# A gated network on one core: silu made on ScalarE directly, in place of a tanh there and one operation on VectorE

## What is computed

```python
x = x + jnp.tanh(g_xattn[0]) * L0_xattn(layernorm(x), ctx)   # RWKV-style weighted scan
x = x + jnp.tanh(g_ffn[0])   * L0_ffn(layernorm(x))
x = x + jnp.tanh(g_xattn[1]) * L1_xattn(layernorm(x), ctx)   # linear attention, sigmoid gate
x = x + jnp.tanh(g_ffn[1])   * L1_ffn(layernorm(x))
# inside L0_ffn: a dense MLP and 8 of 512 product-key experts per token
mlp = silu(x @ gate_w) * (x @ up_w) @ down_w                  # 256 -> 1024 -> 256
ew  = silu(einsum('nh,nkh->nk', x, de)) * softmax(scores)
# inside L1_ffn: 8 routed experts, 2 per token, and a shared one, hidden width 128
h      = silu(rin @ w1[e].T) * (rin @ w3[e].T)
shared = silu(xf @ sw1.T) * (xf @ sw3.T) @ sw2.T
```

## Time and profile before

| | |
|---|---|
| median of 3 runs | 586.26 us (586.02 to 588.57) |
| the profiled execution | 589.14 us, its span 587.3 us |
| mean granted TensorE clock in it | 0.92 |
| busy: PE, DVE, ACT, POOL | 81%, 68%, 30%, 25% of the span |

### The profile page before, as it was taken

One profiled execution on the slowest core, in us unless ns is written; L12 is line 12 of the kernel. 1 busy time (PEld: TensorE's weight loads), 2 busy tenths in 40 slices (PEclk: granted clock), 3 DMA queues, 4 the chain that ended last, 5 costly groups with the idle time before them and its releaser, 6 DMA issues.

```text
span 587.3 us, 7047 instructions
## 1 busy us (share of the span) xinstructions
PE 477.8 (81%) x2142; PEld 367.5 (63%) x2150; DVE 402.3 (68%) x1049; ACT 173.8 (30%) x363; POOL 144.1 (25%) x141
## 2 busy tenths in 40 slices
PE   1755989778999679899999979999868599999720
PEld 1432468656767567668776867777646487888510
DVE  6999777999868997867859683997825343223332
ACT  2601434121233111141222123213334147555210
POOL 4942113551104010000000010000275105004664
PEclk9857999989999889989999989999978699999775
DMA  8150012300000049000000000111121416555653
GB/s 296 69 186 0 2 30 93 94 1 0 2 0 1 1 135 304 1 1 0 2 1 0 2 0 28 54 55 54 64 90 71 127 36 195 165 168 171 180 182 123
DMA packets 34277, 43.79 MB, mean 75 GB/s; under 512 B 3009, under 2 KB 28098, under 8 KB 34242
## 3 DMA queue, kind: packets, MB, share of 16 engines
q1 hardware_dynamic: 31170, 34.96, 18.6%
q0 software_dynamic: 3072, 8.39, 4.7%
HBM read 24.99 MB, written 18.35 MB: 74 GB/s over the span
## 4 chain that ended last, share of the span: by engine, by line
PE 36%; issue 6%; POOL 5%; DVE 4%; DMA 3%; ACT 2%; POOLq 0%; SPq 0%; ACTq 0%; DVEq 0%
PE ring L600 6%; PE acc L564 5%; PE ring L751 3%; PE ring L820 2%; PE ring L767 2%; PE ring L619 2%; PE ring L540 2%; POOL x_rows L1456 2%; PE ring L541 2%; PE ring L542 2%; PE ring L800 2%; POOL q_f L1465 2%; PE ring L584 1%; DMA main_b<-x_rows 1%; PE ring L811 1%
## 5 line engine op out<-in xcount | busy, mean ns | idle before, releaser
L564 PE MATMUL acc<-w_down,act_s 128*128 128x256 f32 x384 | 91.0, 384 | 0.7 <-DVE act_s L1258 0.7
L564 PEld LDWEIGHTS acc<-w_down,act_s 128*128 128x128 f32 x384 | 73.9, 193 | 12.7 <-DVE act_s L1258 1.1
L540 PE MATMUL ring<-xt_h,up_l 128*128 128x512 f32 x160 | 72.3, 452 | 5.4 <-ACT logits L921 3.0
L1426 POOL TENSOR_TENSOR rstd<-var_eps,minus_half 128x4 f32<-128x4 f32 x16 | 16.6, 1035 | 215.5 <-DVE var_eps L1054 215.5
L541 PE MATMUL ring<-xt_l,up_h 128*128 128x512 f32 x160 | 65.0, 406 | 0.0
L542 PE MATMUL ring<-xt_h,up_h 128*128 128x512 f32 x160 | 64.9, 406 | 0.0
L971 ACT ACTIVATE act_s<-ring 128x512 f32<-128x512 f32 x48 | 28.7, 598 | 113.8 <-PE ring L542 113.8
L1241 DVE SCALAR_TENSOR_TENSOR act_s<-act_s,ring 128x512 f32<-128x512 f32 x48 | 32.7, 681 | 29.4 <-ACT act_s L971 22.6
L600 PE MATMUL ring<-up_e,act_s 128*128 x184 | 48.4, 409 | 4.7 <-issue 3.5
L1456 POOL DMA_INDIRECT x_rows<-main_a,slots x32 | 31.5, 985 | 64.5 <-ACT main_a L988 32.4
L600 PEld LDWEIGHTS ring<-up_e,act_s 128*128 128x128 f32 x184 | 35.7, 204 | 11.3 <-issue 6.9
(11 more groups left out here) (239 smaller groups left out, 948.6 us busy)
## 6 DMA issues: line engine op xcount, KB each, us to landing
main_b<-x_rows SPq DMA_DIRECT2D x22, 256.0 KB, 2.9
y_rows<-act_s SPq DMA_DIRECT2D x22, 256.0 KB, 2.2
x_rows<-k_r SPq DMA_DIRECT2D x1, 3968.0 KB, 14.5
x_nat<-in_x SPq DMA_DIRECT2D x8, 256.0 KB, 4.5
stage<-in_w_mlp SPq DMA_DIRECT2D x8, 256.0 KB, 2.7
up_e<-in_w_moe SPq DMA_DIRECT2D x8, 256.0 KB, 2.6
out_x<-x_nat SPq DMA_DIRECT2D x8, 256.0 KB, 2.3
x_rows<-k_r SPq DMA_DIRECT2D x1, 1920.0 KB, 19.7
```

What stands on the lines that cost most here:

```text
L540: pe.matmul(out, wl, xh, start=first, stop=False, skip_group_check=True)
L564: last = pe.matmul(acc[t // 2][:, t % 2, :], act_s[n % RING][:, tok], w_down[:, u, :], start=u == 0 and t % 2 == 0, stop=final, skip_group ...
```

## The change

ACT uses the function Silu on bank A and releases the bank itself; DVE's operation (t + 1) * A is gone in all three places, and with it the halving of the gates. In the units 8 to 11 DVE waits for the silu only ahead of its last multiplication. The semaphores tanh_ready and shared_tanh are gone, since the release of the bank now tells DVE that the silu is written; block_tanh is renamed.

```diff
--- before.py
+++ after.py
@@ -412,20 +412,18 @@
         exp_ready = sem("exp_ready")
         routes_ready = sem("routes_ready")
         exps_high = sem("exps_high")
-        tanh_ready = sem("tanh_ready")
         hid_ready = sem("hid_ready")
         down_done = sem("down_done")
         acc_free = sem("acc_free")
         gate_ready = sem("gate_ready")
         chosen_ready = sem("chosen_ready")
-        shared_tanh = sem("shared_tanh")
         shared_ready = sem("shared_ready")
         slots_ready = sem("slots_ready")
         rows_scaled = sem("rows_scaled")
         rows_cleared = sem("rows_cleared")
         row_sent = [sem(f"row_sent{k}") for k in range(SENDS)]
         blocks_loaded = [sem(f"blocks_loaded{k}") for k in range(4)]
-        block_tanh = sem("block_tanh")
+        block_silu = sem("block_silu")
         y_stored = [sem(f"y_stored{k}") for k in range(2)]
         y_back = [sem(f"y_back{k}") for k in range(2)]
         y_added = sem("y_added")
@@ -968,14 +966,15 @@
                             act.wait_ge(down_done, n - RING + 1)
                         elif n == 0:
                             act.wait_ge(bg_ready, 1)
-                        act.activation(act_s[n % RING][:, :], bank[:, :], ACT.Tanh, scale=0.5).then_inc(tanh_ready, 1)
+                        act.activation(act_s[n % RING][:, :], bank[:, :],
+                                       ACT.Silu).then_inc(free_sem((step, "A", u)), 1)
                         if u == IC:
                             hidden_made(act, n - 1)
                             bank = full(act, (step, "EY"))
                             act.activation(host_s[:, 0, :], bank[:, :], ACT.Copy).then_inc(free_sem((step, "EY")), 1)
                 elif kind == "moe":
                     bank = full(act, (step, "A"))
-                    act.activation(hid_shared[g], bank[:, :], ACT.Tanh, scale=0.5).then_inc(shared_tanh, 1)
+                    act.activation(hid_shared[g], bank[:, :], ACT.Silu).then_inc(free_sem((step, "A")), 1)
                 elif kind == "send":
                     t = part
                     main = t // GT
@@ -1004,8 +1003,8 @@
                             full(act, (("blk", n - 3), "H"))
                         wide = pair_blocks(n - 1)
                         act.activation(hid_blocks[(n - 1) % 2][:, 0:wide * P].rearrange("p (j m) -> p j m", j=wide),
-                                       bank[:, 0:wide * 2 * P].rearrange("p (j m) -> p j m", j=wide)[:, :, 0:P], ACT.Tanh,
-                                       scale=0.5).then_inc(block_tanh, 1)
+                                       bank[:, 0:wide * 2 * P].rearrange("p (j m) -> p j m", j=wide)[:, :, 0:P],
+                                       ACT.Silu).then_inc(block_silu, 1)
                     if 2 <= n <= PAIRS + 1:
                         key = (("blk", n - 2), "H")
                         bank = full(act, key)
@@ -1091,7 +1090,6 @@
                     dve.tensor_tensor(bias_b[:, :], bias_b[:, :], bias_a[:, :], ALU.add).then_inc(dve_setup, 1)
                     dve.wait_ge(act_setup, 2)
                     dve.wait_ge(pool_setup, 1)
-                    dve.tensor_scalar(gates[:, 1::2], gates[:, 1::2], 0.5, None, ALU.mult)
                     for c in range(C):
                         last = dve.tensor_copy(decay[:, c, :].rearrange("p (t j) -> p t j", t=GT)[:, :, 1:],
                                                ew[:, c:c + 1].unsqueeze(2).broadcast_to([P, GT, P]))
@@ -1236,13 +1234,12 @@
                     n = unit_of(g, u)
                     s = act_s[n % RING]
 
-                    dve.wait_ge(tanh_ready, n + 1)
-                    bank = full(dve, (step, "A", u))
-                    free((step, "A", u), dve.scalar_tensor_tensor(s[:, :], s[:, :], 1.0, bank[:, :], ALU.add, ALU.mult))
                     if u >= IC:
                         if u == IC:
                             freed(dve, (step, "EY"))
                         w = host_s[:, 1, :]
+                        if HID_TURN[("mlp", g, u)] > 1:
+                            dve.wait_ge(hid_ready, HID_TURN[("mlp", g, u)] - 1)
 
                         bank = full(dve, (step, "RANK", u))
                         free((step, "RANK", u), dve.scalar_tensor_tensor(w, bank[:, :], float(TOPK), host_s[:, 0, :],
@@ -1253,6 +1250,7 @@
                             bank = full(dve, (step, "OVER"))
                             free((step, "OVER"), dve.tensor_tensor(w, w, bank[:, :], ALU.add))
 
+                        freed(dve, (step, "A", u))
                         for a in range(2):
                             r = slice(a * 2 * P, (a + 1) * 2 * P)
                             last = dve.tensor_tensor(s[:, r].rearrange("p (j h) -> p h j", h=2),
@@ -1329,9 +1328,7 @@
                     dve.wait_ge(chosen_ready, g + 1)
                 elif kind == "moe":
                     a = hid_shared[g]
-                    dve.wait_ge(shared_tanh, g + 1)
-                    bank = full(dve, (step, "A"))
-                    free((step, "A"), dve.scalar_tensor_tensor(a, a, 1.0, bank[:, :], ALU.add, ALU.mult))
+                    freed(dve, (step, "A"))
                     bank = full(dve, (step, "B"))
                     dve.tensor_tensor(a, bank[:, :], a, ALU.mult).then_inc(free_sem((step, "B")), 1)
                     freed(dve, (step, "B"))
@@ -1382,8 +1379,7 @@
                         bank = full(dve, (("blk", n), "U"))
                         both = bank[:, 0:wide * 2 * P].rearrange("p (j w m) -> p j w m", j=wide, w=2)
                         a = hid_blocks[n % 2][:, 0:wide * P].rearrange("p (j m) -> p j m", j=wide)
-                        dve.wait_ge(block_tanh, n + 1)
-                        link(dve.scalar_tensor_tensor(a, a, 1.0, both[:, :, 0, :], ALU.add, ALU.mult))
+                        dve.wait_ge(block_silu, n + 1)
                         dve.tensor_tensor(a, both[:, :, 1, :], a, ALU.mult).then_inc(free_sem((("blk", n), "U")), 1)
                 elif kind == "gather":
                     q = part
```

## The result

Four runs of each kernel: the changed one takes 579.02 us (578.19 to 580.18), the one before 586.68 us (586.02 to 588.57). The medians differ by 7.7 us; the ratio is 0.9859, 95% interval 0.9837 to 0.9881, so 1.4% faster. The forecast was 579.2.

What follows compares the result with a forecast made beforehand. TensorE, 81% busy, was taken to be held up to 410 us by waits on VectorE. Stretch terms -0.9 - 2.9 + 0.8 - 2.1 - 2.0 summed to -7.1 us, taking the median 586.26 to 579.2; range 572 to 596.

Steps and rivals of the forecast that it cites:

- Loads: ScalarE's changes between Exp and Silu: 31 added table loads of 1.28 us, hidden where ScalarE idles, paid where busy.
- 80 to 118, -0.9: Span from 80 to 118 us, first routing: less VectorE work ahead of it, partly offset by a load; net -0.9 us.
- 118 to 146, -2.9: Span from 118 to 146 us: four VectorE operations removed, no function change, TensorE's waits shrink; net -2.9 us.
- no difference: Rival, chance 0.23: TensorE meets the next wait at once, so gains and loads cancel; about 586 us.
- 150 to 201, +0.8: Span from 150 to 201 us, second routing: loads where ScalarE is busy outweigh VectorE's relief; net +0.8 us.
- 201 to 228, -2.1: Span from 201 to 228 us: three TensorE waits shrink by removed VectorE operations and earlier bank release; net -2.1 us.
- 248 to 410, -2.0: Span from 248 to 410 us: TensorE's waits of 3.0, 3.5 and 0.6 us shrink; net -2.0 us.
- From 410, 0: Routed blocks and end: TensorE nearly full, POOL's gathers set the end, so no gain, 0 us.
- The shared table: Rival, chance 0.10: silu sits in Exp's table, no load is added, pure relief of -12.1 us, 574.2 us.
- The drain: On ScalarE, about 1380 ns added to each table load according to the Trainium skill, 2.66 us for a switch.
- the slower outcome: Rival, chance 0.27: ScalarE becomes the link where Exp and silu alternate around 97 to 103 and 174 to 186 us.
- its formula's slope: Where Exp and silu alternate, costlier switches delay VectorE in full: -7.1 + 6 (x - 1.28), x the switch price.

Runs made afterwards that it cites:

- the experiment with ten more: Changed kernel plus ten table loads, made by one-column Silu and Exp activations ahead of five units' silu in the busy ScalarE stretches of stages 1 and 2: 597.59 us, ratio 1.0051.
- the kernel without loads: Changed kernel with Tanh written in place of Silu in units, shared expert and blocks, so no table change occurs: 581.69 us, ratio 0.9788 to the kernel before.
- their own experiment: Kernel before with silu in the shared expert and routed blocks alone, the 48 units keeping tanh and VectorE's operation: 586.67 us, ratio 0.9979.
- the seven mixed units: Changed kernel with seven units standing between Exps kept on tanh and VectorE's operation, 21 new loads: 582.49 us (0.9805), repeated in another set at 577.77 us (0.9828).

## Why the prediction was right, and where it was not

The number, 579.2, stands beside a median of 579.02, and that it meets it so closely is luck: over the four sets the gain is 8.9 us, not 7.1. The mechanism held (relief of VectorE passed on to TensorE, less a price for loads where ScalarE is busy), the sum held as a whole, but by terms that cancel in part. The forecast's -7.1 were waits alone; in the traces TensorE's idle time over the four stages fell by 5.2, and 3.6 more came as shorter busy time, for which the forecast had only an estimate of about 2 us outside its sum.

**Loads: right.** 31 changes were counted and 31 loads are there, of the length of the earlier trace rows. That they run ahead of their activation's wait, argued from one row, is seen at 94.62; that nothing comes on top is seen at 174.62 and in the experiment with ten more. Their price, taken in the sum as 1.3 at the first routing and 3.7 in stage 2 (from -2.9 to +0.8), was 3.4 in all: 0.0 at the first routing, 2.3 in stage 2, and 1.2 in stage 4, which the sum had at nothing.

**80 to 118, -0.9: right in size, by luck.** The term was -2.2 of relief and +1.3 of load; the kernel without loads has the same -0.9, so the relief was smaller and the load cost nothing in the end. Behind it are two halves that I had not seen: the routing's wait fell by 2.3 (4.0 to 1.7, forecast about 3), and the load makes POOL's split late, a new wait of 1.1 us at 111.

**118 to 146, -2.9: the gain of 1.8 has another cause.** Behind the routing's wait TensorE waited 2.0 + 1.5 + 1.4 us before, and 0.6 more at 122.7, 5.5 in all, and 1.6 + 1.6 + 1.5 + 0.5 = 5.2 after: but for 0.3 us the relief was not passed on. Four operations fewer brought TensorE to POOL's split of weights earlier than POOL could make it. This is the rival "no difference", true in this one stretch. What was gained is busy time, 1.5 us: the 4 us at a clock of 0.57 are gone, 4 x 0.43 = 1.7.

**150 to 201, +0.8: +0.4, by two terms that were both too large.** The last silu of the mixed run was put at 186.4 if the stage began as before; it ended at 185.24 in a stage that began 1.4 earlier, so 186.6 by that count. ("Almost without a pause" is not what the timeline of before shows: ScalarE had gaps of 3.75 and 0.92 us there; the sum with 5.6 us of work allowed for them.) The second routing's wait went from 4.7 to 4.9, as said. Without loads it is 4.0 and this part 1.9 shorter than before, not 2.9; the loads cost 2.3, not 3.7. The wait of 1.2 us at 174.6 for line 1241's bank was not in the sum; it became 1.7 with the loads and 0.4 without.

**201 to 228, -2.1: -1.7.** The wait for issue shrank from 2.1 to 1.4, POOL's from 0.9 to 0.7, the bank's 0.7 is gone: 1.6. The clock behind the 4.7 us wait, from which the forecast hoped for something, gave nothing: over this part it was granted at 0.86 before and 0.85 after.

**248 to 410, -2.0: mis-sized; -4.9 measured.** The three waits counted there gave 0.6 + 0.4 + 0.6 = 1.6. In all, TensorE's idle time in the two stages fell by 2.3, near the forecast, and its busy time by 2.5, which the sum had at nothing. What the sum left out of the idle time are short waits in the tails (0.3 for line 1248, 0.7 for the hidden values of line 1258, 0.5 of an "issue"); with the 0.6 above and some busy time these tails became 1.2 and 1.5 shorter. The first part of stage 4 is the error in the other direction: "the attention's changes find ACT idle: 0" missed the load behind the routing's Exp, which costs 1.0 to 1.2; at equal clock the change loses 0.5 there, and the 1.1 gained is clock.

**From 410, 0: wrong.** The blocks, with the shared expert, gain 1.2 (0.4 to 2.1) by their own experiment. A stretch in which TensorE is busy for 50.15 of 52.00 us still has 1.85 to give; a share near full bounds a gain and does not exclude one. The 2.6 that the table shows in the blocks is more than the experiment bears out; the rest of it I put down to the spread of single executions.

**The rivals.** The shared table fell with the count of loads. The drain, and with it the slower outcome, fell with the gap of 0.02 us; its formula's slope held, since added ScalarE time in the mixed runs came through at 12.2 of 15.0. Without any load the forecast's terms made -12.1, and the kernel without loads measured -13.8, part of it clock.

**What stays open:** why the half-clock stretches differ between executions of the same kernel (of the changed kernel's four traces stage 3 has one in three and stage 4 in two, behind waits of the same 2.6 and 2.9 us each time), how much of the gain is therefore clock, whether VectorE's two operations at the first routing were shorter because POOL was idle beside them, and whether the seven mixed units truly win 0.3%.

## What to carry to other kernels

In this kernel a table load cost its bare 1.28 us of ScalarE, and it cost time only where ScalarE had no idle time ahead of the activation that needed it: go along its timeline, and at each change ask whether it idled before and who stands behind the next activation, also a copy that has nothing to do with the function. When work leaves the engine that others wait for, look up what the freed engine meets next (here a third engine's queue), sum the small waits too, and split a gain into idle and busy time of the engine that bounds the stage: here 3.6 of 8.8 us were busy time. An engine at 96% of a stage still leaves the other 4% to be gained.

## What the runs showed of the hardware

Each of the 31 new loads of 1283 ns begins 0.02 us after the activation before it, whether or not its own activation has its input; where the input is there, that activation follows 0.02 us after the load. I had held 2.57 us for a switch to be possible. The 31 loads cost 5.0 us without relief and 3.4 with it, and ten more, placed where ScalarE is busy and each with a one-column activation, cost 12.4: what a load costs depends on what stands around it. With 40 us more on ScalarE its 48 activations stayed at 599 ns each. Where TensorE's wait at the first routing shrank from 4.0 to 1.7 us, a stretch of 4 us at a clock of 0.57 behind it was gone; it is so in all four traces of the changed kernel, but it was not tested by itself, and in stages 3 and 4 equal waits came with and without such a stretch.
